# Two stacked recurrences: one PSUM bank for each gate, biases added with each projection, one product for the low part of the state, and a new prologue

## The reference

```python
xW = jnp.einsum('ntd,dg->ntg', x, Wx) + b
def step(carry, xw_t):                       # layer 0
    prev_h, prev_c = carry
    a = xw_t + prev_h @ Wh                   # Wh: 128 x 512
    i, f, o = sigmoid(three quarters of a); g = tanh(the last quarter)
    next_c = f * prev_c + i * g
    next_h = o * jnp.tanh(next_c)            # c starts at 0, h at cond_1024
def step(h, xt):                             # layer 1
    m = jnp.concatenate([xt, h], axis=-1) @ weight + bias     # weight: 256 x 256
    c = jnp.tanh(m[:, units:]); g = jax.nn.sigmoid(m[:, :units] + 1.0)
    h_new = g * h + (1.0 - g) * c
x = x + layer0(x);  x = x + layer1(x)
```

## Time and profile before

| | us |
|---|---|
| median of 3 runs | 248.27 (247.78 to 248.40) |
| the profiled execution | 247.93 |
| its span, first to last instruction | 246.1 |
| busy: TensorE / VectorE / ScalarE | 229.9 / 224.0 / 130.0 |
| mean granted TensorE clock | 0.973 |

### The profile page before, as it was taken

One profiled execution on the slowest core, in us unless ns is written; L12 is line 12 of the kernel. 1 busy time (PEld: TensorE's weight loads), 2 busy tenths in 40 slices (PEclk: granted clock), 3 DMA queues, 4 the chain that ended last, 5 costly groups with the idle time before them and its releaser, 6 DMA issues.

```text
span 246.1 us, 14402 instructions
## 1 busy us (share of the span) xinstructions
PE 229.9 (93%) x5604; PEld 181.0 (74%) x5604; DVE 224.0 (91%) x1558; ACT 130.0 (53%) x907; POOL 5.6 (2%) x15
## 2 busy tenths in 40 slices
PE   3999999999999999999999999999999999999772
PEld 2777777778787787868778787787777777777672
DVE  6599999999999999999999999999999999999994
ACT  3455555555555555554555545555455555555542
POOL 1700000000000000000000000000000000000000
PEclk9999999999999999999999999999999999999955
DMA  6001010010101001010010101001010100000000
GB/s 216 22 15 39 24 45 14 24 48 13 48 21 32 21 21 43 11 43 21 15 39 21 33 20 43 21 11 43 21 32 21 43 11 21 23 13 15 17 13 11
DMA packets 12260, 7.43 MB, mean 30 GB/s; under 512 B 1478, under 2 KB 11980, under 8 KB 12236
## 3 DMA queue, kind: packets, MB, share of 16 engines
q1 hardware_dynamic: 11936, 6.82, 9.5%
q10 hardware_dynamic: 300, 0.28, 0.3%
HBM read 5.00 MB, written 2.10 MB: 29 GB/s over the span
## 4 chain that ended last, share of the span: by engine, by line
PE 69%; DVE 20%; ACT 6%; issue 3%; DMA 1%; SPq 0%; ACTq 0%
PE a L286 14%; PE fo L261 11%; PE ig L261 6%; PE fo L232 6%; PE ig L232 6%; PE a L277 5%; PE a L237 5%; PE fo L266 5%; DVE cell_bank L496 5%; PE a L280 4%; DVE h_high L503 4%; PE ig L266 4%; ACT act_bank L413 4%; DVE scan_add L489 2%; DVE h_low L508 2%
## 5 line engine op out<-in xcount | busy, mean ns | idle before, releaser
L261 PEld LDWEIGHTS fo<-h_high,wh_part 128*128 128x128 bf16 x762 | 36.4, 96 | 49.1 <-DVE h_high L503 48.8
L403 ACT ACTIVATE act_bank<-fo 128x32 f32<-128x32 f32 x128 | 23.3, 182 | 81.9 <-PE fo L266 81.1
L261 PE MATMUL fo<-h_high,wh_part 128*128 128x32 f16 x762 | 59.3, 179 | 7.5 <-DVE h_high L503 6.9
L266 PE MATMUL fo<-h_low,wh_part 128*128 128x32 f16 x508 | 52.9, 180 | 0.2 <-DVE h_low L508 0.2
L277 PE MATMUL a<-h_high,w1x_part 128*128 128x32 f16 x768 | 45.1, 177 | 0.8 <-DVE h_low L508 0.8
L280 PE MATMUL a<-h_low,w1x_part 128*128 128x32 f16 x512 | 41.9, 177 | 0.0
L496 DVE TENSOR_TENSOR_SCAN cell_bank<-scan_mul,scan_add 128x64 f32<-128x64 f32 x128 | 38.7, 303 | 0.7 <-ACT scan_add L407 0.3
L286 PE MATMUL a<-acts,w1h_part 128*128 128x32 bf16 x768 | 38.7, 177 | 0.0
L261 PE MATMUL ig<-h_high,wh_part 128*128 128x32 f16 x762 | 38.3, 177 | 0.0
L409 ACT ACTIVATE out_gate<-fo 128x32 f32<-128x32 f32 x128 | 25.2, 197 | 20.6 <-PE fo L266 20.6
L277 PEld LDWEIGHTS a<-h_high,w1x_part 128*128 128x128 bf16 x768 | 34.8, 96 | 0.9 <-ACT acts L419 0.9
(11 more groups left out here) (80 smaller groups left out, 489.6 us busy)
## 6 DMA issues: line engine op xcount, KB each, us to landing
xT<-in_x_dram SPq DMA_DIRECT2D x16, 128.0 KB, 2.1
x_add<-in_x_dram SPq DMA_DIRECT2D x32, 64.0 KB, 1.8
out_dram<-outT SPq DMA_DIRECT2D x32, 64.0 KB, 1.6
wx_s<-in_L_cond_Wx_dram SPq DMA_DIRECT2D x1, 256.0 KB, 2.9
wh_raw<-in_L_cond_Wh_dram ACTq DMA_DIRECT2D x1, 256.0 KB, 3.2
w_raw<-in_L_cond_weight_dram SPq DMA_DIRECT2D x1, 256.0 KB, 4.1
bias_rows<-in_biases_dram ACTq DMA_DIRECT2D x1, 3.0 KB
condT<-in_cond_dram ACTq DMA_DIRECT2D x1, 16.0 KB, 3.9
```

The costliest lines, as they stand in the source:

```text
L261: nc.tensor.matmul(gate_step(q, j), wh_part[:, w, q * P:(q + 1) * P], h_high[:, (j - 1) % PARTS, :], start=False, stop=False, skip_group_c ...
L266: mm = nc.tensor.matmul(gate_step(q, j), wh_part[:, w, q * P:(q + 1) * P], h_low[:, (j - 1) % PARTS, :], start=False, stop=w == 1, skip_gr ...
```

## The change

- Each of the four gates has one PSUM bank of its own for 8 steps (`gate_banks`), in place of two pairs. The gates' groups begin at different steps (`BEGIN` = 3, 4, 5, 6 for f, i, g, o); a bank is projected anew at the end of the step that used its last slot, after a wait for ScalarE's (or VectorE's) use of it.
- The bias of a gate is a matmul of its own right behind the projection (256 columns each), `bias0` is gone. In the eight steps of a group the wide work now is: k = 0 the layer-1 bias (512 columns); k = 1 nothing; k = 2, 3, 4, 5 projection and bias of f, i, g, o; k = 6, 7 one half of layer 1's projection each.
- `h_low` is multiplied once with fp16 weights (`wh_fp16`, `w1x_fp16`), in place of twice with bf16 parts. LIFT is 64, not 2048. A step has 36 narrow matmuls.
- The low matmuls of f, i and g stand ahead of the output gate's high ones; the output gate is finished before layer 1, with no wait for the forget sigmoid. Each gate has a semaphore of its own.
- x is loaded once, in half groups of 64 KB (six such chunks are kept), for projections and residual.
- Prologue: 11 matmuls of 256 columns on the identity tile that feed nothing; step 0 does without the forget gate; the other gates are projected for 4, 5 and 6 steps, with bias and first state at once. The splits of layer 1's weight are done by ScalarE between the activations of steps 0 and 1, by GpSimd, and one cast by VectorE.

```diff
-GATE_I, GATE_F, GATE_O, GATE_G = range(4)
+GATE_F, GATE_I, GATE_G, GATE_O = range(4)
...
-LIFT = 2048.0
+BEGIN = (3, 4, 5, 6)
...
+LIFT = 64.0
+FP16_MAX = 65504.0
+WARM = 11
...
+            sp.dma_start(wx_s[:, :], wx).then_inc(wx_in, 16)
+            sp.dma_start(condT[:, :], h_first).then_inc(cond_in, 16)
             load_x(0, 0)
-            sp.dma_start(wx_s[:, :], wx).then_inc(wx_in, 16)
+            load_x(1, 1)
             sp.dma_start(w1_raw[:, :, :], w1.rearrange("(h k) n -> k h n", h=2)).then_inc(w1_in, 16)
-            load_x(1, 1)
-            for slot in range(SLOTS):
-                load_add(slot, slot)
...
+            def project0(q, first, steps=GS):
+
+                k = (first - BEGIN[q]) % GS
+                to = gate_banks[q][:, k * N:(k + steps) * N]
+                nc.tensor.matmul(to, wx_s[:, q * P:(q + 1) * P], xT[:, first * N:(first + steps) * N],
+                                 start=True, stop=False, skip_group_check=True)
+                nc.tensor.matmul(to, bias_lhs[:, :], pick[:, q:q + 1].to_broadcast([P, steps * N]),
+                                 start=False, stop=False, skip_group_check=True)
+
...
-            def bias0(qs, c):
-                both, step = (fo, GATE_O - GATE_F) if qs == (GATE_F, GATE_O) else (ig, GATE_G - GATE_I)
-                to = both[c][:, :].rearrange("p (q n) -> p q n", q=2)
-                row = pick[:, qs[0]:qs[1] + 1:step].unsqueeze(2).to_broadcast([P, 2, GS * N])
-                nc.tensor.matmul(to, bias_lhs[:, :], row, start=False, stop=False, skip_group_check=True)
...
-            def low(q, j, done=None):
-                for w in range(2):
-                    mm = nc.tensor.matmul(gate_step(q, j), wh_part[:, w, q * P:(q + 1) * P],
-                                          h_low[:, (j - 1) % PARTS, :], start=False, stop=w == 1,
-                                          skip_group_check=True)
-                if done is not None:
-                    mm.then_inc(done, 1)
+            def low(q, j, done):
+                nc.tensor.matmul(gate_step(q, j), wh_fp16[:, q * P:(q + 1) * P], h_low[:, (j - 1) % PARTS, :],
+                                 start=False, stop=True, skip_group_check=True).then_inc(done, 1)
...
-                    for w in range(2):
-                        nc.tensor.matmul(to, w1x_part[:, w, q * P:(q + 1) * P], h_low[:, j % PARTS, :],
-                                         start=False, stop=False, skip_group_check=True)
+                    nc.tensor.matmul(to, w1x_fp16[:, q * P:(q + 1) * P], h_low[:, j % PARTS, :],
+                                     start=False, stop=False, skip_group_check=True)
...
+            pe.wait_ge(ident_ready, 1)
+            idle = ident[:, :].bitcast(BF16)
+            for _ in range(WARM):
+                nc.tensor.matmul(a1[1][:, 0:2 * P], idle[:, 0:P], idle[:, :], start=True, stop=True,
+                                 skip_group_check=True)
...
-            for q in (GATE_F, GATE_I, GATE_G, GATE_O):
-                project0(q, 0, q in (GATE_F, GATE_I))
             pe.wait_ge(pick_ready, 1)
             pe.wait_ge(bias_ready, 1)
-            for qs in ((GATE_F, GATE_O), (GATE_I, GATE_G)):
-                bias0(qs, 0)
+            project0(GATE_I, 0, BEGIN[GATE_I])
             pe.wait_ge(wh_in, 16)
             pe.wait_ge(cond_in, 16)
+            first_state(GATE_I, i_summed)
+            pe.wait_ge(x_in[1], 16)
+            project0(GATE_G, 0, BEGIN[GATE_G])
+            first_state(GATE_G, g_summed)
+            project0(GATE_O, 0, BEGIN[GATE_O])
+            first_state(GATE_O, o_summed)
+
+            project0(GATE_F, 1, BEGIN[GATE_F] - 1)
+            pe.wait_ge(w1_gate_ready, 1)
+            project1(0, 0, 0)
+            bias1(0)
...
-                        for q in (GATE_F, GATE_I, GATE_G, GATE_O):
-                            high(q, j)
+                        high(GATE_F, j)
+                        high(GATE_I, j)
+                        high(GATE_G, j)
+                        if first and j == 1:
+                            pe.wait_ge(fp16_ready, 1)
                         pe.wait_ge(low_ready, s)
                         low(GATE_F, j, f_summed)
-                        low(GATE_I, j)
+                        low(GATE_I, j, i_summed)
                         low(GATE_G, j, g_summed)
+                        high(GATE_O, j)
+                        low(GATE_O, j, o_summed)
                         if first and j == 1:
-                            pe.wait_ge(w1_split, 6)
+                            project1(1, 0, 0)
+                            pe.wait_ge(w1_cast, 2)
+                            pe.wait_ge(w1_split, 2)
+                            pe.wait_ge(fp16_ready, 2)
+                            layer1_input(l)
+                            layer1_first()
...
                             pe.wait_ge(acts1_ready, s - 1)
-                        layer1_input(l)
-                        layer1_high(r, l)
-
-                        pe.wait_ge(f_ready, s + 1)
-                        low(GATE_O, j, o_summed)
-                        layer1_rest(r, l)
-                        layer1_low(r, l)
-                    if more:
+                            layer1_input(l)
+                            layer1_high(r, l)
+                            layer1_rest(r, l)
+                            layer1_low(r, l)
...
-                            pe.wait_ge(x_in[other], s0 + 16 * m + 16)
-                            project0(GATE_F, other, True)
-                        if k == 1:
-                            project0(GATE_O, other, False)
-                        if k == 2:
-                            project0(GATE_I, other, True)
-                        if k == 3:
-                            project0(GATE_G, other, False)
-                        if k == 4:
-                            project1(0, other)
-                        if k == 5:
-                            project1(1, other).then_inc(x_projected, 1)
-                        if k == 6:
-                            bias0((GATE_F, GATE_O), other)
-                        if k == 7:
-                            bias0((GATE_I, GATE_G), other)
-                            bias1(other)
+                            bias1(m)
...
+                    ends = last and m == 1
+                    steps = BODY - 1 - j if ends else GS
+                    if k == BEGIN[GATE_F] - 1:
+                        for chunk in (range(3) if m == 0 else range(4, 5)):
+                            if not ends:
+                                pe.wait_ge(x_in[chunk], s0 + 16)
+                        pe.wait_ge(f_ready, s)
+                        project0(GATE_F, j + 1, steps)
+                    if k == BEGIN[GATE_I] - 1:
+                        pe.wait_ge(scan_in_ready, 2 * s + 1)
+                        project0(GATE_I, j + 1, steps)
+                    if k == BEGIN[GATE_G] - 1:
+                        if not ends:
+                            pe.wait_ge(x_in[3 if m == 0 else 5], s0 + 16)
+                        pe.wait_ge(scan_in_ready, 2 * s + 1)
+                        project0(GATE_G, j + 1, steps)
+                    if k == BEGIN[GATE_O] - 1:
+                        pe.wait_ge(o_ready, s + 1)
+                        project0(GATE_O, j + 1, steps)
+                    if k == GS - 2 and not ends:
+                        project1(0, (m + 1) % 2, (m + 1) * GS)
+                    if k == GS - 1 and not ends:
+                        mm = project1(1, (m + 1) % 2, (m + 1) * GS)
+                        if m == 1:
+                            mm.then_inc(ahead_used, 1)
...
+            act.wait_ge(wh_in, 16)
+            nc.scalar.activation(wh_scaled[:, :], wh_raw[:, :], ACT.Copy,
+                                 scale=1.0 / LIFT).then_inc(wh_scaled_ready, 1)
+
+            def split_layer1(part):
+
+                if part == 0:
+                    act.wait_ge(w1_in, 16)
+                    nc.scalar.activation(w1x_scaled[:, 0:P], w1_raw[:, 0, 0:P], ACT.Copy, scale=0.5 / LIFT)
+                    nc.scalar.activation(w1x_scaled[:, P:2 * P], w1_raw[:, 0, P:2 * P], ACT.Copy,
+                                         scale=1.0 / LIFT).then_inc(w1_scaled, 1)
+                if part == 1:
...
+                if part == 2:
+                    act.wait_ge(w1_split, 1)
+                    nc.scalar.copy(w1x_part[:, 1, :], upper(w1x_rest[:, :])).then_inc(w1_cast, 1)
...
+            def gates(s, j, first):
+                if not first:
+                    act.wait_ge(f_summed, s)
+                    gate(forget[:, :], GATE_F, j, ACT.Sigmoid).then_inc(f_ready, 1)
...
+            def keep(s):
+                dve.wait_ge(f_ready, s)
...
+            def scan(s, to, done):
+
+                dve.wait_ge(scan_in_ready, 2 * s + 1)
```

More of the change, by code:

```diff
@@ L571, in body @@
             def body(s0, first):
                 for j in range(BODY):
+                    s = s0 + j
```

(23 more changed lines are left out.)

283 lines of the change are left out of this document (130 added, 153 removed).

## The result

The changed kernel takes 252.66 us (median of 4 runs, 251.80 to 254.03) against 248.03 for the kernel before on the same chip (247.49 to 248.40): 1.0194 times as long, interval 1.0136 to 1.0251. The forecast of 243.5 with its range to 247.5 was wrong. The profiled execution took 251.99 us, its span 250.4, against 247.93 and 246.1.

The account below looks back on a forecast made before the run. The step was taken as bound by a ring through TensorE, ScalarE and VectorE. 247.93 less 2.5 (steady step) less 2.2 (prologue) gave 243.2, with 0.34 for the median 243.5; range 242.0 to 247.5.

Parts of the forecast that it names:

- The step's gain: Steady step: one low forget matmul fewer makes each of 127 steps 0.02 us shorter, 2.5 us (0 to 4.4).
- u_low stands ahead of the scan: VectorE's in-order layer-1 work: u_low cannot move and allows the scan at 122.63 to 122.64, limiting the step's gain to 0.02.
- The clock in the loop: TensorE's granted clock over the loop: taken to stay at 1.00, so falls added nothing to the forecast.
- a rival: Clock falls in some of fifteen stretches around the step without wide matmuls: five falls, 3.0 us, 246.5; chance 0.17.
- both forms: The two clock rivals in the loop: some falls, chance 0.17, and a fall nearly each time, chance 0.12.
- the 0.10 of cover: TensorE's end of step: nine high matmuls in place of twelve end 0.10 before the low ones can start.
- The other rival, a fall nearly each time: Clock falls behind nearly every step without wide matmuls: 15 by 0.8, 12 us and more, 255.5; chance 0.12.
- The gap rule of the Trainium skill: Clock falls come from long idle gaps between matmul bursts; by it neither loop falls. The prediction said the trace disagrees.
- The high matmuls' move: Output gate's three high matmuls go behind the low ones: worth nothing, as the low ones wait for h_low anyway.
- The waits before a projection: TensorE's new waits (forget, scan inputs, output gate) are over by then, and none on x's loads was counted: 0.
- The loop's stall: A VectorE scan in the first of six loop passes starts 0.44 after u_low, not 0.12: 0, plus or minus 0.7.
- The prologue's 2.2: Prologue: first h_high at 7.8 in place of 10.22, gain 2.4, less 0.2 for new meetings: 2.2 (0.8 to 3.0).

Follow-up runs that it names:

- e8: e1 with layer 0's low part multiplied by two bf16 parts again, in place of one fp16 product: 248.07 us.
- e1: Changed kernel plus two 512-column filler matmuls in the one step of eight without a wide matmul (k = 1): 245.11 us.
- e3: Changed kernel, same wide work spread: layer 1's second projection half at k = 0, its bias halved over k = 7 and k = 1: 245.75 us.
- e7: e1 with the output gate's three high matmuls back ahead of the low ones: 247.01 us.
- e6: e1 with the waits for x's chunks moved from ahead of the forget projection to the ends of k = 0 and 1: 244.50 us.
- e4: e3 with 16 warm-up matmuls in the prologue in place of 11: 245.07 us.
- e5: e4 with GpSimd's four layer-1 weight splits on 2 of 256 columns, leaving out those low weight parts: 242.88 us, a single run.
- e2: Kernel before the change, without its bias matmuls in the loop at k = 6 and 7: 252.05 us.
- after: The changed kernel itself, as measured and profiled, against the kernel before: 252.66 us, 1.0194 times as long.
- e9: e3 plus 16 warm-ups, earlier x waits, layer 1's first split earlier on ScalarE, four 512-column fillers in step 1: 242.44 us.
- e10: e9 with 20 warm-up matmuls in place of 16: 242.80 us.

## Why the prediction was wrong, step by step

- **The step's gain: right.** Forecast 0.02 (at most 0.025) from the low forget matmul; measured 0.024 (−3.0 against −2.5), shown by e8. That u_low stands ahead of the scan held it no closer: it too started a little earlier against h_high.
- **The clock in the loop: the step that failed.** The sum put nothing on it ("No cost while TensorE's clock is up"), and the cost stood only in a rival. I named the place, the step without wide matmuls, but held the falls unlikely (0.29 for both forms) because "every neighbouring step is denser than before", and priced them at 0.4 a step, 0.6 a fall, five falls. There were seven, 7.1 us: about 1.0 each, one holding twice as long. e1, which keeps everything else, shows that the falls turned a gain of some 3 into a loss of 4.6: 252.66 becomes 245.11; e3 does it without added work, 245.75. Denser steps next door did not protect seven of the fifteen sparse stretches. Of the size: projection and bias held TensorE for 1.19, some 0.57 more than at full clock (I had 0.48), mostly in two steps a fall, and four of the seven falls met the three waits as well; these took the 0.10 of cover that I had counted on. The other rival, a fall nearly each time, had the direction, but with fifteen falls at 0.8 where there were seven at 1.0.
- **The gap rule of the Trainium skill ("TensorE: Matmul & The Clock Gate", "HAM oscillation"): as weighed.** By long idle gaps nothing would have fallen; seven falls, with no gap over 0.44 in the 4 us before each, say that such gaps aren't needed. I should have let that same row, the tail that fell among narrow matmuls, count for more than the neighbours.
- **The high matmuls' move: right.** It is worth nothing to the forget sum, and its 0.10 of cover, which I counted for the end of step, is real: without it the loop of the trace is 1.4 longer, the median time 1.9 (e7). What I wrote ahead of e7, that the time would stay, left that cover out.
- **The waits before a projection: half right.** None waits for data, but three in a row cost 0.16, seven times: 1.1 (e6), where I had put nothing.
- **The loop's stall, 0 give or take 0.7: it went.** e6 has 0.08 beyond the median over the whole loop, so the stall of the earlier trace rows is gone with the code's new form; why is not shown.
- **The prologue's 2.2: wrong, it was 0.** The output gate's last sum was ready at 8.31, not at 7.0: the first projection started at 4.57, behind the landing of x, and the three gates took 1.1, 1.2 and 1.5 at the low clock, not 1.0 each. So the first h_high gained 1.2, not 2.4. That the clock might rise in time I had as the upper end of the range only, and eleven warm-ups did not raise it; e4 shows that sixteen can, 1.2 at the first h_high. Then VectorE's next instructions met GpSimd's splits, 1.0 (e5), where I had taken 0.2 for all such meetings. The third step took 2.19 for 1.80 before; it is 2.31 in e5 too, so GpSimd is not its cause, and what is was not tested.
- **The terms together.** The span was to fall by 4.7 and grew by 4.3, 9.0 apart: falls 7.1, prologue 2.2, waits 1.1, less 0.5 for the steps, 0.8 for the stall and small excesses of before, and 0.2 for the tail. The falls alone were enough to turn the sign.

Open: why seven of fifteen sparse stretches fell and not all, and why e2, with other sparse stretches, had five, evenly apart. This was not tried. Nor is it known how many falls another execution would have. The runs of after spread over 2.2 us, those of e1 over 1.0, and the longest run of after, 254.03, had the highest mean clock of the four, 0.932, so the number of falls does not explain that spread. Why three of the five kernels with the order of e3 fell once in the loop, at one and the same place, is open too.

## What to carry to other kernels

Where a loop needs TensorE's full clock, look at its sparsest steps, not at its mean: wide matmuls that can run at any time belong in the steps without one, and a kernel can lose by dropping or bundling matmuls. Then read the granted clock over the whole loop again, as even an evenly dealt loop fell once here (e4, e9, e10); the loop with fillers did not (e1, e6, e7, e8). If a trace shows the clock falling anywhere, ask whether the change makes a stretch of the loop look like that one. When instructions are moved off the critical sum, ask what their new place covers at the end of the step.

## What the runs showed of the hardware

- Matmuls of 32 columns alone did not keep the clock: with 72 of them (and the end of a wide one) from 100.00 to 103.50, TensorE busy for 2.77, it fell from 2.4 to 1.2 GHz at 103.50, with no gap over 0.44. Other such stretches of the same loop kept it.
- Eleven matmuls of 256 columns left it low until 11.34 in after (10.36 to 13.76 in e1, e3, e6, e7 and e8); sixteen had it up at 4.85 (e4), 6.39 (e5) and 5.92 (e9), twenty at 6.95 (e10). The kernel before, which has none of them but starts with four projections of 256 columns in a row, had it up at 7.58.
- Three VectorE instructions with two SBUF inputs took 0.52 to 0.66 in place of 0.18 to 0.30, and the cast to fp16 0.70 in place of 0.29, each started while a GpSimd split was under way, while h_high, with one input in PSUM, started beside a split at 9.05 and stayed at 0.19.
- Three satisfied waits in a row on TensorE cost 0.16, seen where no other work covers them (e6).
